# TensorE waits for its input tile by tile instead of for the whole input

## The reference

```python
xa  = ln(x)                                    # normed over channels
sx  = shift(xa) - xa                           # the position before, minus this one
xxx = xa + sx * maa_x
t   = tanh(xxx @ maa_w1).reshape(B, L, 5, -1)  # the "ranks"
mw, mk, mv, mr, mg = einsum(t, maa_w2)
xw, xk, xv, xr, xg = (xa + sx * (maa_j + mj) for j in "wkvrg")
w = exp(-exp(time_decay + tanh(xw @ decay_w1) @ decay_w2))      # the "decay"
r, k, v, g = xr @ Wr.T, xk @ Wk.T, xv @ Wv.T, silu(xg @ Wg.T)   # projections
y = group_norm(scan over the 256 positions of k, v, w, r)       # state 16 x 16 in each of 32 heads
x = x + y * g @ Wo.T
xc, sxc = ln(x), shift(ln(x)) - ln(x)
xk2, xr2 = xc + sxc * fmaa_k, xc + sxc * fmaa_r
x = x + sigmoid(xr2 @ fWr.T) * (relu(xk2 @ fWk.T) ** 2 @ fWv.T)
```

## Time and profile before

| | us |
|---|---|
| median of three runs | 872.62 |
| lowest, highest | 872.28, 875.66 |
| the profiled execution | 872.65 |
| its span (first to last instruction) | 870.6 |
| TensorE busy (PE) | 812.5 (93%) |
| VectorE busy (DVE) | 601.7 (69%) |
| ScalarE busy (ACT) | 354.2 (41%) |
| GpSimd busy (POOL) | 295.6 (34%) |

### The profile page before, as it was taken

The page is one execution under the profiler, slowest core; times in us unless marked ns, Lnnn a source line. Parts: engine busy times, 40 slices in busy tenths (PEclk is TensorE's granted clock), DMA queues, the critical chain, the costliest instruction groups (busy, mean ns, idle before and its releaser), DMA issues. The chain is left out here.

```text
span 870.6 us, 18064 instructions
## 1 busy us (share of the span) xinstructions
PE 812.5 (93%) x7370; PEld 542.1 (62%) x7370; DVE 601.7 (69%) x1110; ACT 354.2 (41%) x715; POOL 295.6 (34%) x281
## 2 busy tenths in 40 slices
PE   7799999799999999899998899989999899999997
PEld 4477568447664676447764577636775377457764
DVE  2475867896579836896389944898369976894441
ACT  1322336524562327424364144633364157225512
POOL 3043741383118510383106720185103921540000
PEclk9899999999999999999999999999999999999999
DMA  9830103000110001100011001100001000100000
GB/s 300 328 97 1 49 2 123 1 2 1 26 49 2 1 26 50 49 1 1 26 50 49 2 2 48 51 25 1 2 1 48 27 2 2 49 1 3 26 24 24
DMA packets 17026, 34.20 MB, mean 39 GB/s; under 512 B 2224, under 2 KB 3888, under 8 KB 16944
## 3 DMA queue, kind: packets, MB, share of 16 engines
q1 hardware_dynamic: 14048, 31.20, 10.4%
q10 hardware_dynamic: 2896, 1.86, 0.7%
HBM read 24.66 MB, written 8.39 MB: 38 GB/s over the span
## 5 line engine op out<-in xcount | busy, mean ns | idle before, releaser
L2061 POOL TENSOR_TENSOR xmix<-xmix,xa 128x512 f32<-128x512 f32 x80 | 94.1, 1197 | 172.8 <-DVE xmix L1567 172.8
L2074 POOL TENSOR_TENSOR prod<-RA,K 128x512 f32<-128x512 f32 x112 | 126.7, 1157 | 23.6 <-DVE RA L1631 20.7
L1240 ACT ACTIVATE st<-av,half 32x512 f32<-32x512 f32 x64 | 74.7, 1166 | 43.3 <-DVE av L1714 41.9
L625 PE MATMUL CH<-prod,ones 32*32 32x512 f32 (+1 forms) x1152 | 75.8, 582 | 10.2 <-DVE av L1661 8.9
L1661 DVE TENSOR_TENSOR av<-CH,vT 128x512 f32<-128x512 f32 x112 | 71.7, 681 | 12.5 <-PE CH L625 12.3
L1567 DVE SCALAR_TENSOR_TENSOR xmix<-PA,chan,sx 128x256 f32<-128x256 f32 x128 | 52.9, 475 | 39.0 <-PE PA L509 37.5
L1672 DVE TENSOR_REDUCE yred<-av 128x64 f32<-128x512 f32 (+2 forms) x112 | 70.9, 674 | 0.0
L718 PE MATMUL PC<-sq_Wo,y 128*128 128x512 f32 x128 | 61.5, 612 | 6.6 <-DVE y L1757 6.6
L525 PE MATMUL PC<-sqb,sq_fWk 128*128 128x256 f32 x256 | 60.6, 386 | 6.4 <-DVE sqb L1793 6.4
L2086 POOL TENSOR_TENSOR K<-K,W 128x512 f32<-128x512 f32 x8 | 15.3, 1915 | 143.4 <-DVE prod L1597 143.4
L525 PE MATMUL PB<-xmix,sq_Wk 128*128 128x256 f32 x256 | 61.7, 386 | 0.0
(11 more groups left out here) (163 smaller groups left out, 1388.4 us busy)
## 6 DMA issues: line engine op xcount, KB each, us to landing
x<-x_rows SPq DMA_DIRECT2D x11, 512.0 KB, 3.4
x<-in_x SPq DMA_DIRECT2D x8, 512.0 KB, 3.7
x_rows<-x SPq DMA_DIRECT2D x8, 512.0 KB, 4.2
out_x<-x SPq DMA_DIRECT2D x8, 512.0 KB, 2.8
ctx_t<-in_ctx SPq DMA_DIRECT2D x5, 512.0 KB, 3.8
y<-in_ctx SPq DMA_DIRECT2D x3, 512.0 KB, 8.3
sq_Wk<-in_square SPq DMA_DIRECT2D x1, 1024.0 KB, 13.5
sq_Wv<-in_square SPq DMA_DIRECT2D x1, 1024.0 KB, 16.9
```

The source lines that it names most:

```text
L625: mm = pe.matmul(out, ones16[rows, rows], v, start=True, stop=True)
L1240: act.activation(st[p, :, :, 32 * q:32 * q + S], src, ACT.Copy, scale=half[p, 0:1]).then_inc(st_ready, 1)
L2061: pool.tensor_tensor(m, m, xa[:, ct:ct + 2, 1:L + 1], ALU.add).then_inc(mix_ready, 1)
L2074: pool.tensor_tensor(by_pair(prod[:, g % 4, :], h), r, k, ALU.mult).then_inc(prod_pool, 1)
```

## The change

Nothing is computed differently and no instruction changes its place on any engine. What changes is which matmul waits for which count.

- `a_ranks` waits for one count of `xxx_ready` before each of its first four matmuls.
- `a_decay` and the projections wait before matmul `kt` for the pair of `xmix` tiles that it reads. The projections do so for the first output tile only.
- `c_key` waits for one tile of `sqb` before each matmul of the first output tile, and `c_receptance` for the two tiles of `sxc` that each of its parts reads.
- DVE counts `xk2_ready` and `xr2_ready` after each tile. ScalarE's one wait for `xr2_ready` (`c_sig`) gets the new total.

```diff
 def a_ranks(a):
-    pe.wait_ge(xxx_ready, CT * (a + 1))
     if a:
         pe.wait_ge(gate_ready, 2 * a)
     ...
     for kt in range(CT):
+        pe.wait_ge(xxx_ready, CT * a + kt + 1)
         pe.matmul(PB[:, 512:768], maa_w1[:, kt, 0:P], zbuf[:, kt * L:(kt + 1) * L], ...)

-def columns_tile(out, mt, w, rhs, signal):
+def columns_tile(out, mt, w, rhs, signal, ready, values):
     for kt in range(CT):
+        if mt == 0:
+            pe.wait_ge(ready, values[kt])
         mm = pe.matmul(out[:, mt * L:(mt + 1) * L], w[:, kt, mt * P:(mt + 1) * P], rhs[:, kt, :], ...)

 def a_decay(a):
-    pe.wait_ge(mix_ready, 10 * a + 2)
     pe.wait_ge(mix_scaled, 10 * a + 4)
     for kt in range(CT):
+        pe.wait_ge(mix_ready, 10 * a + 1 + kt // 2)
         for th in range(TT):
             mm = pe.matmul(PB[DD * th:DD * (th + 1), 0:P], dec_w1[:, kt, :], xmix[:, 0, kt, th * P:(th + 1) * P], ...)

 def a_key(a, mt):
     if mt % 2 == 0:
-        pe.wait_ge(mix_ready, 10 * a + 4)
         pe.wait_ge(decay_exp, 4 * a + mt + 2)
     ...
-    columns_tile(PB, mt, sq_w["Wk"], xmix[:, 1], k_mm)
+    columns_tile(PB, mt, sq_w["Wk"], xmix[:, 1], k_mm, mix_ready, [10 * a + 3 + kt // 2 for kt in range(CT)])
 ...
 def c_key(c, mt):
-        pe.wait_ge(xk2_ready, c + 1)
     ...
-    columns_tile(PC, mt, sq_w["fWk"], cols(sqb[:]), fk_mm)
+    columns_tile(PC, mt, sq_w["fWk"], cols(sqb[:]), fk_mm, xk2_ready, [CT * c + kt + 1 for kt in range(CT)])

 def c_receptance(c, t, part):
     if part == 0:
-        pe.wait_ge(xr2_ready, c + 1)
         pe.wait_ge(relu_ready, 2 * c + t + 1)
     ...
+    pe.wait_ge(xr2_ready, CT * c + 2 * part + 2)
     rows_part(PC, t, part, sq_w["fWr"], sxc, fr_mm)

 def c_shift(c):        # DVE; c_shift_r has the same edit with xr2_ready
     for ct in range(CT):
-        i = dve.scalar_tensor_tensor(sqb[:, ct * L:(ct + 1) * L], sxc[:, ct, :], vec("fmaa_k", ct), ...)
-    i.then_inc(xk2_ready, 1)
+        dve.scalar_tensor_tensor(sqb[:, ct * L:(ct + 1) * L], ...).then_inc(xk2_ready, 1)
```

More of the change, by code:

```diff
@@ L573, in a_value @@
                 if mt % 2 == 0:
-                    pe.wait_ge(mix_ready, 10 * a + 6)
                     pe.wait_ge(K_ready, 2 * a + mt // 2 + 1)
@@ L577, in a_value @@
                         pe.wait_ge(wv_centred, 1)
-                columns_tile(PB, mt, sq_w["Wv"], xmix[:, 2], v_mm)
+                columns_tile(PB, mt, sq_w["Wv"], xmix[:, 2], v_mm, mix_ready, [10 * a + 5 + kt // 2 for kt in range(CT)])
             def a_receptance(a, mt):
@@ L583, in a_receptance @@
                 if mt % 2 == 0:
-                    pe.wait_ge(mix_ready, 10 * a + 8)
                     pe.wait_ge(vT_ready, 2 * a + mt // 2 + 1)
@@ L587, in a_receptance @@
                         pe.wait_ge(w_sq["Wr"], 16)
-                columns_tile(PB, mt, sq_w["Wr"], xmix[:, 0], r_mm)
+                columns_tile(PB, mt, sq_w["Wr"], xmix[:, 0], r_mm, mix_ready, [10 * a + 7 + kt // 2 for kt in range(CT)])
             def a_gate(a, mt):
@@ L593, in a_gate @@
                 if mt % 2 == 0:
-                    pe.wait_ge(mix_ready, 10 * a + 10)
                     pe.wait_ge(R_ready, 2 * a + mt // 2 + 1)
@@ L597, in a_gate @@
                         pe.wait_ge(w_sq["Wg"], 16)
-                columns_tile(PB, mt, sq_w["Wg"], xmix[:, 1], g_mm)
+                columns_tile(PB, mt, sq_w["Wg"], xmix[:, 1], g_mm, mix_ready, [10 * a + 9 + kt // 2 for kt in range(CT)])
             def b_chunks(u, lo, hi):
@@ L1292, in c_sig @@
                     return
-                act.wait_ge(xr2_ready, c + 1)
+                act.wait_ge(xr2_ready, CT * (c + 1))
                 for t in range(TT):
@@ L1792, in c_shift @@
                 for ct in range(CT):
-                    i = dve.scalar_tensor_tensor(sqb[:, ct * L:(ct + 1) * L], sxc[:, ct, :], vec("fmaa_k", ct),
-                                                 xc[:, ct, 1:L + 1], ALU.mult, ALU.add)
-                i.then_inc(xk2_ready, 1)
+                    dve.scalar_tensor_tensor(sqb[:, ct * L:(ct + 1) * L], sxc[:, ct, :], vec("fmaa_k", ct),
+                                             xc[:, ct, 1:L + 1], ALU.mult, ALU.add).then_inc(xk2_ready, 1)
             def c_shift_r(c):
@@ L1801, in c_shift_r @@
                 for ct in range(CT):
-                    i = dve.scalar_tensor_tensor(sxc[:, ct, :], sxc[:, ct, :], vec("fmaa_r", ct), xc[:, ct, 1:L + 1],
-                                                 ALU.mult, ALU.add)
-                i.then_inc(xr2_ready, 1)
+                    dve.scalar_tensor_tensor(sxc[:, ct, :], sxc[:, ct, :], vec("fmaa_r", ct), xc[:, ct, 1:L + 1],
+                                             ALU.mult, ALU.add).then_inc(xr2_ready, 1)
             def c_out(c, t):
```

## The result

The changed kernel takes 871.19 us (median of 21 runs, 868.12 to 875.28), the kernel before in the same comparison 872.89 (872.01 to 875.66, 21 runs). The ratio is 0.9979, interval 0.9969 to 0.9989. By the ratio that is 1.8 us less, where the sum had 4.8. The forecast was 867.9 with 865.8 to 870.4, so it missed, while most of the gain that it describes is in the trace, row by row. The profiled execution took 873.87 us, 871.9 of it in the span.

What follows compares the result with a forecast made beforehand. TensorE, busy 812.5 of 870.6 us, was taken as the bound, so only its waits could be won: 2.5 + 1.1 + 0.15 + 0.95 = 4.7, say 4.8, from 872.65 to 867.9 us, range 865.8 to 870.4.

Steps and rivals of the forecast that it cites:

- the sum: All expected gains together over the whole kernel: 4.7 us, say 4.8.
- c_key in an iteration: c_key of batches 0 to 4 ends 1.19 us earlier; POOL's product leaves 0.50 each, 2.5 in all.
- Batch 7: Last c_key, in the drain: starts at 844.05 in place of 845.07, 1.1 us gained with the pace.
- Batch 6: c_key in the drain: could gain 1.19 us, but the turning of K waits for av, so 0.0.
- batch 6's rest: A small remainder for c_key of batch 6 in the drain, taking the total from 4.7 to 4.8 us.
- Decay: Decay's split wait: 0.0 in the iterations, where DVE's scaling of k still holds it; 0.15 us in the fill.
- Ranks: Ranks of batch 0, in the fill: start at 35.34 in place of 36.19, 0.95 us counted whole.
- The price of the waits: The 144 added waits and DVE's 48 added counts cost zero; upper end 0.216 us a wait.
- The step that failed: Semaphore instructions at places with two conditions: two conditions there before too, so the skill's rule leaves the sum unchanged.
- The clock: Rival: the slow-clock stretch after batch 2's ranks may go, 1.5 us more, 866.4, or another may come; chance 0.14.

Runs made afterwards that it cites:

- e1: The kernel before, unedited, timed again: 872.95 us, ratio 0.9997.
- e5: The changed kernel with the dropped wait for mix_ready put back at output tile 2 of the four projections: 868.37 us, ratio 0.9939.
- e10: The changed kernel with second, long-met waits on 26 matmuls behind 796 us, in batch 7: 870.76 us, ratio 0.9981.
- e9: The changed kernel with second, long-met waits on 28 matmuls of batch 0's Wk and Wv projections: 870.38 us, ratio 0.9971.
- e6: The kernel before without the redundant wait for mix_ready at output tile 2 of the projections, waits kept whole: 875.25 us, ratio 1.0026.
- e3: The kernel before with only c_key's wait split tile by tile: 870.06 us, ratio 0.9967.
- e7: The kernel before with only the waits of c_key and of the ranks split, instruction count as before: 868.94 us, ratio 0.9955.
- e11: e5 with POOL making its product for chunk 16 ahead of its mix 2, TensorE's order kept: 865.35 us, ratio 0.9911.
- e4: The changed kernel, but each of c_key's four waits asks for the last tile of sqb: 874.71 us, ratio 1.0014.

## Why the prediction missed

**c_key in an iteration: right.** 0.51 each. From the end of batch 0's ranks to the 5500th matmul, in batch 6's work near 640, e1 takes 604.22 and e5 601.04. The difference of 3.18, taken matmul by matmul, is 5 x 0.5, 0.2 in the fill behind the ranks, 0.36 at a small stall near 522 that e1 has (the profile of before has it too, 0.27 at 523.24, also at a border), and 0.1 in small steps. **Batch 7: right**, by the start of `c_key`, 1.03 and 0.10 for the pace. Batch 6 gave 0.0, as its paragraph said; the 0.1 "with batch 6's rest" that makes 4.8 of 4.7 has no row behind it.

**Decay: right.** From e1 to e5 it gained 0.10 in batch 0 and 0.10 in batch 1, and nothing that lasts in the iterations: 0.2 where 0.15 was taken.

**Ranks: right only in part of the executions.** The 0.95 is there when the fill starts early. Where TensorE comes to L439 at 35.0, the ranks follow 1.07 later with whole waits (the profile of before) and 0.22 later with split ones (e10). But in ten of the 14 profiles the fill is held up ahead by 1.2 or more, and then `zbuf` is ready: in e1, whole waits, L439 is at 36.57 and the ranks follow 0.22 later as well. One profile had shown an early start, and I took it for all. So this term of the sum, 0.95, is 0 in most of the profiles.

**The price of the waits: right as far as it went.** Split waits cost nothing in pace (3.62 for 16 records; 7.17 for 32 with 14 more semaphore instructions between them, e9), and so do the 48 counts on DVE.

**The step that failed** stands in the paragraph behind it: "The new waits have one condition each where a matmul had none, and the places with two had two before, so the rule would leave the sum as it is". Output tile 2 of the projections lost its second condition. I listed what was added and not what fell away. The Trainium skill ("Perfetto Trace Analysis", section Identifying Dependency Chains) says that an instruction which waits on several engines may get EventSemaphore instructions ahead of it; with one condition fewer that one goes, and the trace agrees, 298 became 269. So the price of the waits, zero in the sum, left out what the change does to the instruction stream. What no rival had is that fewer instructions could cost time. e6 gives the price of this one side effect in the kernel before, 2.6 us. e5, without it, has 868.37, 0.5 from the forecast, but that nearness is in part luck. In the profiles e5's span is 5.7 shorter than e1's: 2.5 + 1.1 + 0.2 are terms of the sum, the ranks gave nothing, 0.4 is the small stall near 522, and 1.3 was won near 680, where e1 is at the lower clock level from 676.84 to 683.67.

**The clock** was a rival, with 0.14 to the good side, "or another may come". The other came. Two measures of its share follow. The first goes by matmuls. The profile of the changed kernel is 6.5 longer than e5's. The first stall and the slow stretch behind it are 2.74 of that (1.06 and 1.68), the second 2.30, the lower level from 676.93 to 683.75 is 1.2, and the rest lies ahead of the ranks. The lower level took half of its 6.8 us there and cost only 1.2, for e5 waits for POOL at the end of the same stretch:

```profile
683.68 1.09 PE L632 MATMUL CH<-prod,ones 32*32 32x512 f32 x16 [2.13 <-POOL prod L2078]
```

The second goes over all runs, by span and mean clock: span x clock is the span less half of the time at the lower level. By the place near 680 it counts more than the level costs. The changed kernel (21 runs, mean) has 860.2 and 9.1 lost, e5 (5 runs) 859.5 and 6.4, before (25 runs) 863.0 and 7.8, e6 (12 runs) 864.8 and 8.8. So of the 3.4 us between the changed kernel and e5 at most 2.7 is clock, and 0.7 or more is the stalls' own time. The stalls of the profiled execution, 2.0, are longer than that, and the fastest five of its 21 runs, 868.12 to 868.49, have a clock of 0.992 to 0.994 where the profiled one has 0.986: not every run loses what the profiled one lost. Of e5's gain of 4.9 in the span, at least 3.5 is idle time gone and up to 1.4 is less time at the lower level, which I can't tell from chance with 5 runs; the profiles of e3, e5, e7, e10 and e11 have full clock around 680, the other nine don't. Why is open.

Also open is why a packet comes late, as in four of the ten stalls. Of the changed kernel's program the border of batch 5 stalls in two profiles and passes in e4 and e10, whose stream is the same up to there: in e10 a packet began at 614.2, in the first profile none between 609.3 and 619.0. Something delays the request, and no run here shows what. That the stalls of other runs look like those of the profiled ones is an inference from the medians.

## What to carry to other kernels

A whole wait may hide another one: split, it gives only the part up to the hidden one (here POOL's product), and the rest comes when that is moved too, as in e11. Count what an edit takes away as well as what it adds, by the instruction total at the head of the page, and look for idle time under "issue" in long runs of small matmuls before blaming the edit for a loss. Look at more than one profiled execution for what happens at the start.

## What the runs showed of the hardware

- TensorE's instructions arrive in packets of 16,384 bytes (58 or 59 in a run), by count 256 records each. The first of a packet never ran earlier than 2.24 us after the packet had begun to arrive. 128 matmuls of 32 rows with their weight loads take 1.68 us (e5), so that such a run can overtake the supply: ten stalls of 0.8 to 1.3 us in seven of 14 profiles, and a stretch at the lower clock level begins within 1.1 us of eight of these ten.
- Semaphore instructions whose condition is met cost no time between matmuls: 28 among 32 matmuls (64 records) of Wk and Wv in e9, 7.17 us for each of the two groups, as in e5 without them.
- 28 such instructions fewer made the kernel before 0.26% slower (e6, 1.0014 to 1.0039).
